# Pair dot products carried from PSUM to the matmul's rows inside SBUF, by rectangular blocks

## What is computed

```python
bot_out = _mlp(dense_x, [bw0, bw1, bw2], ...)                  # 13 -> 512 -> 256 -> 128
gathered = stack([emb[t][sparse_x[:, t]] for t in range(26)])  # 26 rows of 128 each
features = concatenate([bot_out[:, None, :], gathered], axis=1)  # 27 x 128 per sample
Z = einsum('bnd,bmd->bnm', features, features)
interact = Z[:, LI, LJ]                                        # the 351 pairs i > j
x = concatenate([bot_out, interact], axis=1)
return _mlp(x, [tw0, tw1, tw2, tw3, tw4], ...)                 # 479 -> 1024 -> 1024 -> 512 -> 256 -> 1
```

## Time and profile before

| | |
|---|---|
| median of three runs (lowest, highest) | 180.82 us (180.34, 181.10) |
| span of the profiled execution, first to last instruction | 179.6 us |
| PE, ACT, DVE, POOL busy | 167.0, 66.3, 82.2, 100.7 us |
| mean granted TensorE clock, share of full speed | 0.991 |
| pieces on the path: pairs from scratch, scratch from dots | 3% and 3% of the span |

### The profile page before, as it was taken

One profiled execution on the slowest core, in us unless ns is written; L12 is line 12 of the kernel. 1 busy time (PEld: TensorE's weight loads), 2 busy tenths in 40 slices (PEclk: granted clock), 3 DMA queues, 4 the chain that ended last, 5 costly groups with the idle time before them and its releaser, 6 DMA issues.

```text
span 179.6 us, 3315 instructions
## 1 busy us (share of the span) xinstructions
PE 167.0 (93%) x1354; PEld 128.6 (72%) x1354; DVE 82.2 (46%) x177; ACT 66.3 (37%) x103; POOL 100.7 (56%) x112
## 2 busy tenths in 40 slices
PE   1999999899599994999999999989999999999993
PEld 1335557568377783798878889977888898788992
DVE  3202588955165756374452346343506625411422
ACT  0576748664143655133033253112504611110211
POOL 3777776777777777777777777767772000000000
PEclk9999999999999999799999999999999999999999
DMA  4999972434499733242232244422223120000000
GB/s 97 369 337 391 390 239 58 100 66 89 89 302 374 285 79 86 54 100 68 44 61 51 52 105 85 93 46 62 46 59 72 24 53 7 4 0 0 0 0 4
DMA packets 10124, 19.93 MB, mean 111 GB/s; under 512 B 5639, under 2 KB 5771, under 8 KB 9981
## 3 DMA queue, kind: packets, MB, share of 16 engines
q1 hardware_dynamic: 6636, 12.89, 22.0%
q0 software_dynamic: 3328, 6.82, 16.7%
q10 hardware_dynamic: 144, 0.00, 0.0%
HBM read 18.26 MB, written 1.44 MB: 110 GB/s over the span
## 4 chain that ended last, share of the span: by engine, by line
PE 71%; DMA 10%; POOL 8%; issue 4%; SPq 2%; DVE 2%; ACT 2%; POOLq 0%; DVEq 0%; ACTq 0%
PE acc L799 14%; PE acc L803 13%; PE acc L800 12%; POOL rows L420 8%; PE feat L781 6%; PE turned L944 5%; PE feat L763 5%; DMA rows<-in_emb,index 3%; PE turned L881 3%; DMA pairs<-pair_scratch 3%; DMA pair_scratch<-dots 3%; PE acc L829 2%; PE acc L938 2%; PE feat L938 2%; DMA v<-in_bw 1%
## 5 line engine op out<-in xcount | busy, mean ns | idle before, releaser
L420 POOL DMA_INDIRECT rows<-in_emb,index x104 | 99.5, 957 | 34.4 <-issue 30.0
L799 PE MATMUL acc<-w1h,y_split 128*128 128x512 f32 x64 | 27.9, 436 | 0.0
L803 PE MATMUL acc<-w1h,y_split 128*128 128x512 f32 x64 | 26.1, 407 | 0.0
L800 PE MATMUL acc<-w1l,y_split 128*128 128x512 f32 x64 | 25.5, 399 | 0.0
L444 ACT COPY featT<-feat 128x512 f32<-128x512 f32 x16 | 17.6, 1097 | 14.4 <-PE feat L763 14.3
L457 ACT ACTIVATE y_split<-turned 128x512 fp32r<-128x512 f32 x16 | 9.7, 606 | 35.1 <-PE turned L881 35.1
L651 DVE SCALAR_TENSOR_TENSOR y_split<-turned,y_split 128x512 fp32r<-128x512 f32 x16 | 11.1, 692 | 18.7 <-ACT y_split L457 18.7
L799 PE MATMUL acc<-w2h,y_split 128*128 128x256 f32 x64 | 18.8, 294 | 0.0
L803 PE MATMUL acc<-w2h,y_split 128*128 128x256 f32 x64 | 18.0, 281 | 0.0
L763 PE MATMUL feat<-ident,rows 128*128 128x128 f32 x104 | 15.3, 277 | 2.7 <-DMA rows<-in_emb,index 2.7
L800 PE MATMUL acc<-w2l,y_split 128*128 128x256 f32 x64 | 17.8, 279 | 0.0
(11 more groups left out here) (107 smaller groups left out, 255.6 us busy)
## 6 DMA issues: line engine op xcount, KB each, us to landing
w1r<-in_w SPq DMA_DIRECT2D x8, 512.0 KB, 13.8
w2r<-in_w SPq DMA_DIRECT2D x4, 512.0 KB, 6.0
rows<-in_emb,index POOLq DMA_INDIRECT x104, 3.0
w0r<-in_w_pairs SPq DMA_DIRECT2D x3, 512.0 KB, 7.8
top<-in_top_rows SPq DMA_DIRECT2D x1, 1024.0 KB, 12.1
pair_scratch<-dots SPq DMA_DIRECT2D x8, 104.0 KB, 2.3
pair_scratch<-dots SPq DMA_DIRECT2D x8, 71.5 KB
v<-in_bw SPq DMA_DIRECT2D x1, 512.0 KB, 3.6
```

What stands on the lines that cost most here:

```text
L420: pool.indirect_dma_start(rows[:, i, :], None, table, bass.IndirectOffsetOnAxis(ap=index[:, c, i:i + 1], axis=0)).then_inc(s_gather[LOTS * ...
L799: nc.tensor.matmul(dst, ah, wh, start=first, stop=False)
L800: nc.tensor.matmul(dst, ah, wl, start=False, stop=False)
L803: return nc.tensor.matmul(dst, al, wh, start=False, stop=end)
```

## The change

The trip through HBM goes away. `BLOCKS` lists rectangles (n0, ns, m0, ms): features n0 to n0+ns-1 by features m0 to m0+ms-1. A transfer moves one rectangle from `dots` straight into ns x ms rows of `pairs`. Some rows of the rectangles are pairs that stand elsewhere or a feature with itself; their weights are zero. The tiles have 126, 117 and 127 rows (plus the bias row) in place of 117 each. Tile 0 takes one transfer, tile 1 seven, tile 2 five. Tiles 0 and 1 are issued by SP, tile 2 by ACT inside `dots_out`, after a wait for the copies of both engines. `dots` keeps 27 columns in place of 26. All eight bursts of products use single samples.

```diff
+BLOCKS = (
+    ((14, 9, 0, 14),),
+    ((7, 7, 0, 7), (18, 5, 14, 4), (4, 3, 0, 4), (11, 3, 7, 4), (5, 2, 4, 2), (12, 2, 11, 2), (19, 4, 18, 4)),
+    ((0, 24, 23, 4), (24, 2, 25, 2), (1, 3, 0, 3), (8, 3, 7, 3), (15, 3, 14, 3)),
+)
...
+        def block_rows(eng, h, i):
+            row = 0
+            for n0, ns, m0, ms in BLOCKS[i]:
+                eng.dma_start(pairs[row:row + ns * ms, i, h * HALF:(h + 1) * HALF],
+                              dots[HALF * h + n0:HALF * h + n0 + ns, m0:m0 + ms, :]).then_inc(s_pin[h][i], 16)
+                row += ns * ms
...
-            def scratch_out(c, h):
+            def pairs_back(c, h):
                 sp.wait_ge(s_za, HALVES * c + h + 1)
                 sp.wait_ge(s_zd, HALVES * c + h + 1)
...
-                sp.dma_start(scratch[h, 0:FIRST_ROWS], dots[low:mid]).then_inc(s_scr0[h], 16)
-                sp.dma_start(scratch[h, FIRST_ROWS:], dots[mid:low + FEATS]).then_inc(s_scr1[h], 16)
...
+                block_rows(sp, h, 0)
+                block_rows(sp, h, 1)
...
             def dots_out(c, h):
...
                 nc.scalar.copy(*dot_quadrant(h, 1)).then_inc(s_za, 1)
+                if (c, h) == (0, 0):
+                    act.wait_ge(s_one, 1)
+                after(act, s_xlp, PAIR_TILES * c)
+                act.wait_ge(s_za, HALVES * c + h + 1)
+                act.wait_ge(s_zd, HALVES * c + h + 1)
+                block_rows(act, h, PAIR_TILES - 1)
...
-                (sample_pairs if half < HALVES * CHUNKS - 1 else single_samples)(h)
...
                 for g in range(GROUPS):
                     for q in range(QUADS):
                         sample = featT[:, h, QUADS * g + q, 0:FEATS]
```

More of the change, by code:

```diff
@@ L40 @@
 BANK_GROUPS = GROUPS // BANKS
-HOPS = (FEATS - 1) // 2
 PAIR_TILES = 3
[L43 to L46, removed]
+BLOCKS = (
[3 more added lines that the diff above has]
+)
+PAIR_ROWS = [sum(n * m for _, n, _, m in blocks) for blocks in BLOCKS]
+TILE_ROWS = [PAIR_ROWS[0], PAIR_ROWS[1], PAIR_ROWS[2] + 1]
+PINS = [16 * len(blocks) for blocks in BLOCKS]
 B0, B1, B2 = 512, 256, 128
@@ L52 @@
 SMALL = 8
[L55 to L72, removed]
 def pair_weights(w, bias):
     out = np.zeros((PAIR_TILES, P, w.shape[1]), w.dtype)
-    for at, (a, b) in enumerate(pair_order()):
-        out[at // PAIR_ROWS, at % PAIR_ROWS] = w[DIM + a * (a - 1) // 2 + b]
-    out[PAIR_TILES - 1, PAIR_ROWS] = bias
+    placed = set()
+    for i, blocks in enumerate(BLOCKS):
+        row = 0
+        for n0, ns, m0, ms in blocks:
+            for n in range(n0, n0 + ns):
+                for m in range(m0, m0 + ms):
+                    a, b = max(n, m), min(n, m)
+                    if a != b and (a, b) not in placed:
+                        placed.add((a, b))
+                        out[i, row] = w[DIM + a * (a - 1) // 2 + b]
+                    row += 1
+    assert len(placed) == FEATS * (FEATS - 1) // 2
+    out[PAIR_TILES - 1, PAIR_ROWS[PAIR_TILES - 1]] = bias
     return out
@@ L98, in after, with rec_kernel @@
         eng.wait_ge(sem, count)
-def rec_kernel(nc, x_turned, sparse, emb, bw, small, w0_bot, w0_pairs, w1, w2, w3_in, top_rows, scratch, out):
+def rec_kernel(nc, x_turned, sparse, emb, bw, small, w0_bot, w0_pairs, w1, w2, w3_in, top_rows, out):
     with ExitStack() as ctx:
@@ L146, in rec_kernel @@
             h0T = sb("h0T", [P, B0 // P, BATCH], F32, early)
-        dots = sb("dots", [P, COLS, HALF])
+        dots = sb("dots", [P, FEATS, HALF])
         y2h = sb("y2h", [P, T2 // P, P], F32R)
@@ L265, in dot_quadrant @@
             block_ = feat[QUAD * q:QUAD * q + FEATS, :].rearrange("n (g c) -> n c g", c=GROUP_COLS)
[L266 removed]
+            return dots[HALF * h:HALF * h + FEATS, :, at:at + GROUPS], block_[:, q * FEATS:(q + 1) * FEATS, :]
+        def block_rows(eng, h, i):
+            row = 0
+            for n0, ns, m0, ms in BLOCKS[i]:
+                eng.dma_start(pairs[row:row + ns * ms, i, h * HALF:(h + 1) * HALF],
+                              dots[HALF * h + n0:HALF * h + n0 + ns, m0:m0 + ms, :]).then_inc(s_pin[h][i], 16)
+                row += ns * ms
         FIRST_PACED = 36
@@ L446, in dots_out @@
             def dots_out(c, h):
-                after(act, s_scr0[h], 16 * c)
-                after(act, s_scr1[h], 16 * c)
+                for i in range(PAIR_TILES):
+                    after(act, s_pin[h][i], PINS[i] * c)
                 act.wait_ge(s_z, HALVES * c + h + 1)
@@ L461, in pairs_hi @@
                 for h in range(HALVES):
-                    act.wait_ge(s_pin[h][i], (16 if i < PAIR_TILES - 1 else 32) * (c + 1))
+                    act.wait_ge(s_pin[h][i], PINS[i] * (c + 1))
                 after(act, s_l[0], 2 * c)
-                nc.scalar.copy(xh[0:PAIR_ROWS + 1, i, :], pairs[0:PAIR_ROWS + 1, i, :]).then_inc(s_xhp, 1)
+                nc.scalar.copy(xh[0:TILE_ROWS[i], i, :], pairs[0:TILE_ROWS[i], i, :]).then_inc(s_xhp, 1)
             def layer2_out(c, half):
@@ L616, in dots_out @@
             def dots_out(c, h):
-                after(dve, s_scr0[h], 16 * c)
-                after(dve, s_scr1[h], 16 * c)
+                for i in range(PAIR_TILES):
+                    after(dve, s_pin[h][i], PINS[i] * c)
                 dve.wait_ge(s_z, HALVES * c + h + 1)
@@ L1087 @@
                aps["in_small"], aps["in_w0_bot"], aps["in_w0_pairs"], aps["in_w1"], aps["in_w2"], aps["in_w3"],
-               aps["in_top_rows"], scratch, out)
+               aps["in_top_rows"], out)
     result = run(nc, [arrays], core_ids=[0])
```

32 lines of the change are left out of this document (4 added, 28 removed).

## The result

| | before | after |
|---|---|---|
| median (lowest to highest), same chips | 180.96 us (180.34 to 181.6) | 204.91 us (204.3 to 206.78) |
| span of the profiled execution | 179.6 us | 202.5 us |

The ratio is 1.1329, with a 95% interval of 1.1257 to 1.1401. The kernel became slower by 24 us, where I had forecast 3. The direction was right; the size was far outside my range.

A forecast was written before the change was run, and what follows sets the result against it. PE bounds the kernel (167.0 of 179.6 us), POOL's gathers pacing it until 71.69. 6.24 + 0.44 - 2.68 - 0.52 - 0.47 = +3.01 us gives 183.8 us; forecast's own range 182 to 186.5, wider range 180.4 to 187.8.

The forecast's parts named there:

- The bursts of products: Single samples cut a burst on PE from 1.87 to 1.20 us; four bursts count in full, 2.68 us saved.
- Gather 20: Start-up gather idle 0.82 us for the first burst, usually 0.30; a shorter burst gives 0.52 us back to the gathers.
- The path of the pairs: At the boundary between chunks 1 and 2, one round in place of two removes PE's idling: minus 0.47 us.
- Tile 1's landing is hidden: Seven SP transfers land 7.8 us after the burst's end; ACT's delay hides this, without it some tenths would bind.
- ACT's five issues: They hold ACT 2.65 us ahead of its split; PE loses 2.08 us at each of three boundaries, 6.24 in all.
- upper bound: If an issue's cost goes by the source's features, the large block takes 2.05 us and ACT's five issues 4.1.
- Between the bursts: ACT's lots queue behind its issues, 0.22 us longer from burst to burst; 0.44 us for chunks 2 and 3.
- The start-up absorbs: ACT's delay of about a microsecond and tile 1's later landing are covered by PE's wait for gathers at 71.69.
- The clock: Within the much slower rival: granted clock falls to 0.58 after PE's waits, 1.3 us per boundary, 3.8 us more, 187.6.
- much slower: Rival, chance 0.12: either ACT's issues take 4.1 us (191 us) or the clock falls (187.6); range 186.5 to 192.
- The faster one: Rival, chance 0.14: issues leave ACT free, POOL's last gather limits the gain to 1.7 us; 179.4 us (179 to 179.9).
- POOL's pace: POOL's gathers set the pace up to PE's wait at 71.69 us; after that PE does, closely followed by POOL.

The follow-up runs named there:

- r2: The kernel before with all eight bursts by single samples, pairs still through HBM: 182.31 us beside 181.31, ratio 1.0028.
- r1: The changed kernel with seven of the eight bursts by two samples per matmul again: 207.9 us, ratio 1.1482.
- r5: r3 with six of tile 1's seven transfers left out as well (part of the work left out): 180.57 us beside 181.34, ratio 0.9991.
- r3: The changed kernel with ACT's five transfers left out everywhere, SP's eight kept (part of the work left out): 191.36 us, ratio 1.0559.
- r8: The kernel before with seven transfers of different forms added in a row near its end, each waited for: 126 rows cost 0.84 us, 4 rows 0.71.
- r9: The changed kernel with ACT's five transfers issued in chunk 0 alone, left out in chunks 1 to 3: 195.62 us.
- r11: The kernel before with all bursts by single samples and POOL's gathers of chunks 1 to 3 left out: 177.29 us, ratio 0.9785.
- r12: The changed kernel with POOL's gathers of chunks 1 to 3 left out: 199.84 us, ratio 1.1051.
- r10: The kernel before with POOL's gathers of chunks 1 to 3 left out (78 of 104): 176.99 us, ratio 0.9788.

## Why the prediction missed

What I had decide the case, ACT's issues ahead of its split, was the mechanism at the boundaries, and there its price was too low. The largest error was another one, the step that the start-up absorbs every delay. Of the 19.9 us by which the span was missed, 9.0 lie in the start-up, 7.2 in the three boundaries and 3.8 between the bursts. In the order of my steps:

- **The bursts of products: 0.67 us from each, 2.68 in all.** Failed. I carried the last burst's 1.20 us over to bursts with gathers beside them. They took 1.7 to 2.3. By itself the edit gave nothing (r2). Within the changed kernel the old bursts were some 3 us worse (r1), in a stretch where the clock was low and not in the bursts. Gather 20 sat idle for 0.59 us, so of the 0.52 us that it should have given back, 0.23 came.
- **The path of the pairs: minus 0.47 us.** Right in the number, -0.49 in the table, and one round does give it where a tile takes one transfer (r5). With seven transfers for tile 1 it came only because `layer0` was 3.3 us later: without that delay the same stretch holds a wait of 2.57 us (r3). That is luck.
- **Tile 1's landing is hidden.** Right at the three boundaries of the changed kernel, where PE does not wait for it, but by a wide miss in both numbers. I had it land 6.3 us after the dots; measured in the start-up it is 7.93, nearly all of it because the issues behind the first two cost 0.65 to 0.76 us in place of 0.45. And I had it bind by "some tenths" without ACT's delay; it binds by 1.24, 2.57 and 1.56 us (r3). Taking ACT's issues away therefore uncovers a second cost, 10.8 us with what comes with it (r3 less r5).
- **ACT's five issues: 2.65 us.** Mis-sized: 3.9 us at each boundary. My upper bound was near it, though for another reason, the features of the source (and its terms, 2.05 + 4 x 0.45 + 4 x 0.04, make 4.0 and not 4.1). I took 0.45 us by the size of a transfer; the price goes by its form (r8). At three boundaries this makes 3 x 1.26 = 3.8 us more, between the bursts 2 x 1.26 = 2.5.
- **Between the bursts: 0.22 us.** With the measured issues it is 1.48, and the burst by single samples gave some 0.05 us back, not 0.67. That makes 1.43; 1.47 and 1.39 were measured.
- **The start-up absorbs.** Failed, and it is the largest error: +8.46 us where I had -0.52. I wrote that no pacing point of POOL is near enough to ACT's delay. One gather paced by a lot stood still for 4.37 us and one paced by `layer0` for 3.29, so the wait for gathers that was to absorb the delay moved with it. The error is in the part for ACT's issues (6.1 us by the fourth burst with those of chunk 0, r9); tile 1's landing by itself was absorbed, as I had said (r3).
- **The clock.** I had it as a rival at 1.3 us per boundary. It came at the last boundary (1.3 us), at the sixth burst (0.41) and in much of the start-up, on top of the waits.

The boundaries add up: predicted 4.90, plus 3.78 for issues, 1.34 for the two bursts that stayed long, 0.41 for the sixth burst at the lower clock and 1.3 for the last boundary make 11.7 of 12.09; the eighth burst, 1.40 us in place of 1.20, is 0.2 more.

Of the rivals, "much slower" named both causes that came, but as either one or the other, and with a chance of 0.12, and neither had a loss in the start-up. The faster one is refuted: five starts took 3.9 us of ACT, and removing them from all halves took 13.5 us off the kernel. Its rule from the Trainium skill, "DMA: Bandwidth & Descriptors", section "Issuing engines are not separate DMA queues" (what an engine spends on starting a transfer is usually small beside the transfer), does not hold for transfers of this size: an issue took 0.31 to 0.84 us of the 1.7 to 2.5 until the transfer had landed (r8).

No version tried here that does all the work is faster than the kernel before; r2 only equals it.

## What to carry to other kernels

Count the instructions that issue DMAs, not their bytes: a block transfer of 4 rows took 0.71 us of its queue and one of 126 rows 0.84, so cutting one strided pattern into many rectangles multiplies the price. Every transfer in the line also puts off the landing of the last one. In an engine that also computes, put issues behind the work that another engine waits for: the same five issues behind the split gave back 7.4 us. And before a delay is called absorbed, follow the engine that is waited for as well: here POOL was paced by the very lots that came late.

## What was not expected of the hardware

- A row of 128 small matmuls runs in 1.2 us when no gather is in flight, and is broken by pauses of 0.19 us, to 1.7 and more, when gathers are (r11 and r12 against r2 and the changed kernel); once it was held for 2.25 us without any (r11).
- Leaving out 78 gathers makes the kernel before only 4 us faster (r10), and 3.5 of these are won by the fourth burst, where the prediction saw POOL's pace end.
- The granted clock fell after a wait of 1.48 us ahead of a burst, but not after one of 1.41 us at the boundary behind it.
